# The skip term as a product with a diagonal on TensorE, the gate product on VectorE, the weighing of x on GpSimd, in a Mamba-2 block

## The chip, the cores and the metric

One core of one Trainium2 chip runs the whole program. The metric is device time in microseconds. The engines are PE (TensorE), DVE (VectorE), ACT (ScalarE), POOL (GpSimd) and SP (SyncE, which here only issues DMAs); each works off its own queue in order, and semaphores tie them together.

## The reference

The input is 8 sequences of 512 tokens with 128 channels. What matters here is the Mamba part:

```
x    = rmsnorm(layernorm(h));  proj = x @ in_proj_w          # z, xBC, dt
xBC  = silu(causal depthwise conv of width 4 over xBC)
xs   = x part, 32 heads of 64;  B, C: 8 groups of 64 states
dt   = softplus(dt_raw + dt_bias);  dA = exp(-exp(A_log) dt)
h_t  = dA_t h_(t-1) + (dt_t x_t) B_t ;   y_t = h_t . C_t
y    = y + D * xs                                            # the skip term
g    = y * silu(z);  g = g * rsqrt(mean(g^2) over groups of 256 + eps)
out  = residual + (g * gate_norm_w) @ out_proj_w
```

A feed-forward part with ternary weights, GELU and two layer norms follows. The change doesn't touch it.

## The kernel before, in words

A batch is one sequence. Its 2048 inner channels are 16 tiles of 128 channels (two heads of 64 each) by 512 tokens. The program works in slots, 16 to a batch and one for each such tile, four to a unit (r = 0 to 3). All the engines run the same slots with a function `slot(b, n)` each, and a tile passes through them with lags: projected and convolved, then four slots later transposed, scanned and its gate projected (`LAG_SSD`), after five its decays and matrices are made on POOL (`LAG_M`), after six its chunk states are built (`LAG_STATE`), after seven its y (`LAG_Y`), after eight the skip term, gate and square (`LAG_SUM`), then the norm, and after fifteen the out projection (`LAG_OUT`). Batches 1 to 6 run in a hardware loop (`Fori`); the first and the last ones are written out. Slots with r = 1 and 2 project two convolution tiles, those with r = 0 and 3 one (`PLAN`), and every slot projects one gate tile z. Each projection is three passes of 512 columns (`three_passes`, high and low parts).

In a slot PE does half of the transposes of x, the state products of the even blocks (`states(0)`, 64x64 tiles), the first projection, the other transposes, `states(1)`, then small transposes that differ by slot: C times B into `cbs` at r = 0, B into `bt` at r = 1, the norm factor into `rbs` at r = 2, the next batch's input in slot 7 and the result in slot 15 (`XN_SLOT`, `XO_SLOT`). Then, in an order that depends on the slot, a second projection if there is one, y within the blocks (`y_intra`, 32 records), the out projection, the variance at r = 0, the gate projection, and y from the states (`y_inter`, 28 records). The waits for y (`y_inputs`) are placed before the last pass of a two-tile slot's second projection, and before the out projection in the other slots.

DVE does the skip term (`skip`: D times x plus y, from PSUM, two instructions, one for the even and one for the odd blocks), the scan that makes the decay matrix `lm`, the weighing of x for the states (`weigh`: `xw`, out of PSUM), and then seven steps of the state recurrence (`state_step`) interleaved with the three convolution taps of each tile (`ORDER`). The state products of the next slot on PE wait for the last step. ACT starts each convolution (`start_tile`), ends it with SiLU (`finish_tile`), copies PSUM to SBUF, makes `xdt` (x times dt, eight pieces), the gate's SiLU and the square. POOL multiplies `lm` by `cbs`, y by the gate, makes `cdec`, applies the norm factor and sums squares. SP reloads `spread` (the decays, spread over partitions) when `cdec` has read it.

`y_bank[e]` are two PSUM banks; their left half holds y, their right half (`spare`) the small transposes. The ring of `lm` has eight places.

## Time and profile before

| | us |
|---|---|
| median of 3 runs | 1373.94 (1372.95 to 1377.06) |
| the profiled execution | 1385.78 |
| its span | 1384.0 |
| busy: PE / DVE / POOL / ACT | 1127.0 / 1080.2 / 897.2 / 789.1 |
| mean granted TensorE clock | 0.927 of full speed |

Busy time is the union of an engine's instructions in the profiled execution; it counts neither waits nor the issue of DMAs. Matmuls overlap one another in the records, so the time that PE needs for a group is read from the start of the group to the start of the next.

### The profile page before, as it was taken

To read this page: it belongs to the slowest core of one execution; us is meant where nothing else is said; L and a number is where in the kernel's file an instruction comes from. 1 tells how busy PE (TensorE), PEld (TensorE's weight loads), DVE (VectorE), ACT (ScalarE), POOL (GpSimd) and SP (SyncE) were. 2 spreads that over 40 slices of the span, in tenths; PEclk is the share of its full clock that TensorE was granted. 3 is DMA by queue.
4 is the path that set the end of the run, shared out by engine and by line. 5 is a ranking of instruction groups with operands and counts; after the bars stand their busy time and mean duration, and the time that the engine had idled before them with its cause. 6 is when DMAs were issued, how large, how long until landed. Compare 5 with 4: busy or idle time off the path is not lost. (4 is left out here: it accounts for less than half of the span.)

```text
span 1384.0 us, 43524 instructions
## 1 busy us (share of the span) xinstructions
PE 1127.0 (81%) x15222; PEld 772.6 (56%) x15222; DVE 1080.2 (78%) x2325; ACT 789.1 (57%) x2090; POOL 897.2 (65%) x848
## 2 busy tenths in 40 slices
PE   2447889888889879888989798979898999887687
PEld 1324666565556556555656566646565666553455
DVE  7737898887788868885888588868887888656895
ACT  2635666665566646663666466646665666542443
POOL 1632478786687758775878487857786788694231
PEclk9975899998999989997999799989999999896999
DMA  5432123222222222221322122222221321201211
GB/s 140 153 87 58 48 69 86 63 65 63 63 72 62 63 60 87 58 70 51 81 65 64 57 78 63 63 71 73 57 73 50 91 63 63 70 25 40 100 30 31
DMA packets 88881, 94.40 MB, mean 68 GB/s; under 512 B 22736, under 2 KB 66384, under 8 KB 88400
## 3 DMA queue, kind: packets, MB, share of 16 engines
q1 hardware_dynamic: 84432, 89.37, 22.9%
q8 instruction: 133, 2.18, 0.6%
q10 hardware_dynamic: 4224, 2.10, 0.5%
q14 instruction: 92, 0.75, 0.2%
HBM read 81.99 MB, written 9.44 MB: 66 GB/s over the span
## 5 line engine op out<-in xcount | busy, mean ns | idle before, releaser
L1067 DVE SCALAR_TENSOR_TENSOR conv<-bank,cw,conv 128x511 f32<-128x511 f32 (+2 forms) x576 | 426.8, 741 | 38.4 <-ACT conv L764 37.8
L764 ACT ACTIVATE conv<-bank,cb_bias,cw 128x512 f32<-128x512 f32 x192 | 149.1, 777 | 196.6 <-PE bank L1294 196.6
L619 POOL TENSOR_TENSOR gated<-gated,gate 128x512 f32<-128x512 f32 x128 | 163.8, 1280 | 100.6 <-DVE gated L1029 99.5
L864 ACT ACTIVATE xdt<-bank,dt_all 128x64 f32<-128x64 f32 x1024 | 222.4, 333 | 0.0
L1081 DVE SCALAR_TENSOR_TENSOR hpk<-hpk,pend,bank 128x64 f32<-128x64 f32 x768 | 210.4, 274 | 9.9
L1364 PE MATMUL bank<-gated,w_out 128*128 128x512 f32 x256 | 156.2, 695 | 63.8 <-ACT cbs L799 20.0
L612 POOL TENSOR_TENSOR lm<-lm,cbs 128x512 f32<-128x512 f32 x128 | 163.6, 1278 | 48.9 <-ACT cbs L799 37.0
L640 POOL TENSOR_TENSOR ssum<-ssum,sq 128x512 f32<-128x512 f32 x96 | 122.7, 1278 | 88.4 <-ACT sq L845 88.4
L1029 DVE SCALAR_TENSOR_TENSOR gated<-chan,dskip,bank 128x256 f32<-128x256 f32 x256 | 110.8, 474 | 88.1 <-PE bank L1484 80.1
L634 POOL TENSOR_TENSOR gated<-gated,rbs 128x512 f32<-128x512 f32 x128 | 163.7, 1280 | 13.2 <-ACT rbs L814 13.0
L1290 PE MATMUL bank<-xn_hi,w_hi 128*128 (+1 forms) x320 | 165.9, 518 | 7.3 <-PE bank L1473 3.3
L1342 PE MATMUL bank<-xw,bt 64*64 64x64 f32 x3584 | 167.7, 233 | 0.0
L629 POOL TENSOR_TENSOR cdec<-spread,chan 128x512 f32<-128x512 f32 x128 | 163.9, 1280 | 0.0
L1056 DVE TENSOR_TENSOR xw<-bank,wt_all 128x512 f32<-128x512 f32 x128 | 88.4, 690 | 91.5 <-PE bank L1375 88.8
L1342 PEld LDWEIGHTS bank<-xw,bt 64*64 64x64 f32 x3584 | 131.5, 141 | 46.8 <-issue 46.4
L1294 PE MATMUL bank<-xn_hi,w_lo 128*128 (+1 forms) x320 | 137.6, 430 | 22.3 <-DVE hpk L1081 13.4
L1043 DVE TENSOR_TENSOR_SCAN lm<-spread,bank 128x512 f32<-128x512 f32 x128 | 155.0, 1211 | 0.0
L1375 PE MATMUL bank<-ident_t,chan 128*128 128x128 f32 x512 | 108.7, 296 | 55.5 <-ACT xdt L864 22.1
L1484 PEld LDWEIGHTS bank<-cdec,hpk 64*64 64x64 f32 x3584 | 119.1, 139 | 59.4 <-issue 57.5
L1484 PE MATMUL bank<-cdec,hpk 64*64 64x64 f32 x3584 | 136.7, 226 | 0.5
L1291 PE MATMUL bank<-xn_lo,w_hi 128*128 (+1 forms) x320 | 133.0, 416 | 0.0
L784 ACT ACTIVATE chan<-conv 128x512 f32<-128x512 f32 x192 | 121.0, 630 | 19.3 <-issue 8.5
(175 smaller groups left out, 1613.7 us busy)
## 6 DMA issues: line engine op xcount, KB each, us to landing
spread<-decay_scratch SPq DMA_DIRECT2D x256, 128.0 KB, 3.3
spread<-product_scratch SPq DMA_DIRECT2D x256, 128.0 KB, 3.8
lm<-in_L_attn_in_proj_w SPq DMA_DIRECT2D x1, 2048.0 KB, 8.6
xn_scratch<-chan SPq DMA_DIRECT2D x4, 512.0 KB, 5.0
r_stage<-residual_scratch SPq DMA_DIRECT2D x8, 256.0 KB, 2.7
x_scratch<-r_stage SPq DMA_DIRECT2D x8, 256.0 KB, 3.6
cbs<-x_scratch SPq DMA_DIRECT2D x8, 256.0 KB, 3.0
gated<-x_scratch SPq DMA_DIRECT2D x1, 2048.0 KB, 8.9
```

The source lines that it names most:

```text
L612: gp.tensor_tensor(lm[:, at, :], lm[:, at, :], cbs[:, v % 2, :], ALU.mult).then_inc(m_done, 1)
L619: gp.tensor_tensor(gated[:, v % 2, mr, :], gated[:, v % 2, mr, :], gate[:, mr, :], ALU.mult).then_inc(gated_done, 1)
L629: gp.tensor_tensor(cdec[:, mr, :], spread[:, mr, 1, :], chan[:, chan_of(v, 1), :], ALU.mult).then_inc(cdec_done, 1)
L634: gp.tensor_tensor(gated[:, v % 2, m % R, :], gated[:, v % 2, m % R, :], rbs[:, :], ALU.mult).then_inc(normed, 1)
L864: act.activation(xdt[:, r, at:at + HP], xt_bank[:, at:at + HP], ACT.Copy, scale=dt_h).then_inc(xdt_done, 1)
L1043: V.tensor_tensor_scan(lm[:, m % (2 * R), :], spread[:, m % R, 0, :], seed_bank[:, :], 0.0, ALU.mult, ALU.add).then_inc(scanned, 1)
L1067: V.scalar_tensor_tensor(out=conv[:, ci % 4, shift:S], in0=tile_bank(b, n, t)[:, 0:S - shift], scalar=cw[:, q, t, KW - 1 - shift:KW - shif ...
L1081: V.scalar_tensor_tensor(out=hpk[:, m % 2, k, :], in0=hpk[:, m % 2, k - 1, :], scalar=pend[:, m % R, k:k + 1], in1=s_bank[:, NS * k:NS * k ...
L1290: MM(dst, wh, hi, start=True, stop=False)
L1342: last = MM(s_bank[half, NS * (2 * c + e):NS * (2 * c + e) + NS], bt[rows_e, c, half], xw[rows_e, m % R, P * c + HP * a:P * c + HP * a + H ...
L1364: MM(out_bank[:, :], w_out[:, m, :], gated[:, (m // R) % 2, m % R, :], start=(m == 0), stop=(m == SLOTS - 1)).then_inc(out_step, 1)
L1484: last = MM(y_bank[e][half, BLK * c:BLK * c + BLK], hpk[half, m % 2, k - 1, :], cdec[half, m % R, BLK * k:BLK * k + BLK], start=False, sto ...
```

## The change

The skip term becomes two fp32 matmuls on PE (`y_skip`, between `y_intra` and `y_inter`), with a diagonal matrix of D as the weights, one of 16, which ACT makes once in batch 0 and which lie in the upper half of `lm`; so the ring of `lm` has four places. DVE multiplies y in PSUM by the gate (`gate_y`) instead of adding the skip term, and POOL's gate product goes. POOL makes `xw` from `xdt` instead of DVE from PSUM, one slot later than before. The weight `wt_all` isn't multiplied by dt any more. PE's order becomes: out projection, all transposes of x, `states(0)`, first projection, `states(1)`, variance, small transposes, then the second projection or the gate projection with `y_inputs` before its last pass, `y_intra`, `y_skip`, `y_inter`, and the gate projection where it has not been done. ACT and POOL get new orders, SP waits for `pend`, and the scaling of the out weights moves from before the slots into batch 0.

```diff
-
-ORDER = {0: "0123456", 1: "0T12T34T56", 2: "0T1T2T3T4T56T"}
...
+        diag = lm[:, R:2 * R, :].rearrange("p a s -> p (a s)").rearrange("p (m d) -> p m d", d=P)
...
-                after(sp, cdec_done, SLOTS, b, m - R)
+                after(sp, pend_done, SLOTS, b, m - R)
...
-                    after(gp, scanned, SLOTS, bb, m)
-                    after(gp, cb_copied, 2 * UNITS, bb, 2 * v + 1)
-                    after(gp, spread_loaded[mr], 64 * UNITS, bb, 64 * v + 63)
-                    state_there(gp, bb, m - R)
-                    at = m % (2 * R)
-                    gp.tensor_tensor(lm[:, at, :], lm[:, at, :], cbs[:, v % 2, :], ALU.mult).then_inc(m_done, 1)
-                if yy is not None:
...
-                    after(gp, gate_done, SLOTS, bb, m)
-                    skip_there(gp, bb, m)
-                    gp.tensor_tensor(gated[:, v % 2, mr, :], gated[:, v % 2, mr, :], gate[:, mr, :], ALU.mult).then_inc(gated_done, 1)
...
-                    gp.tensor_copy(pend[:, mr, :].unsqueeze(2),
-                                   spread[:, mr, 1, :].rearrange("p (k i) -> p k i", i=BLK)[:, :, BLK - 1:BLK]).then_inc(pend_done, 1)
+                        gp.wait_ge(dtstep_a, 7)
+                    after(gp, scanned, SLOTS, bb, m)
+                    after(gp, spread_loaded[mr], 64 * UNITS, bb, 64 * v + 63)
                     after(gp, silu_done, NCONV, bb, CONV_ORDER.index((v, 1)))
                     after(gp, y_ready, SLOTS, bb, m - R)
                     gp.tensor_tensor(cdec[:, mr, :], spread[:, mr, 1, :], chan[:, chan_of(v, 1), :], ALU.mult).then_inc(cdec_done, 1)
+
+                    xdt_there(gp, bb, m)
+                    after(gp, s_ready, SLOTS, bb, m - R)
+                    wt_b = (wt_all[:, bass.ds(bb * CH, CH), 8 * v + mr:8 * v + mr + 5:4]
+                            .unsqueeze(3).broadcast_to([P, CH, 2, HP]))
+                    gp.tensor_tensor(xw[:, mr, :].rearrange("p (c a d) -> p c a d", c=CH, a=2),
+                                     xdt[:, mr, :].rearrange("p (c a d) -> p c a d", c=CH, a=2),
+                                     wt_b, ALU.mult).then_inc(xw_done, 1)
...
-                if yy is not None and yy[1] % R > 0:
-
-                    bb, m = yy
-                    after(gp, sq_done, SLOTS, bb, m)
-                    after(gp, ssum_step, 3 * UNITS, bb, 3 * (m // R) + m % R - 2)
-                    gp.tensor_tensor(ssum[:, m // R % 2, :], ssum[:, m // R % 2, :], sq[:, :], ALU.add).then_inc(ssum_step, 1)
...
+                if yy is not None and yy[1] % R > 0:
...
+                    after(gp, cb_copied, 2 * UNITS, bb, 2 * v + 1)
+                    state_there(gp, bb, m - R)
+                    gp.tensor_tensor(lm[:, mr, :], lm[:, mr, :], cbs[:, v % 2, :], ALU.mult).then_inc(m_done, 1)
+                    gp.tensor_copy(pend[:, mr, :].unsqueeze(2),
+                                   spread[:, mr, 1, :].rearrange("p (k i) -> p k i", i=BLK)[:, :, BLK - 1:BLK]).then_inc(pend_done, 1)
...
+            def scale_weights(n):
+
+                if n == 0:
+                    act.wait_ge(wo_loaded, 16 * 2 * UNITS)
+                    act.wait_ge(small_loaded, NSMALL * 16)
+                act.activation(w_out[:, n, :], w_out[:, n, :], ACT.Copy, scale=gnw[:, n:n + 1]).then_inc(wo_scaled, 1)
+                if n == 5:
+                    act.wait_ge(wlo, 4 * UNITS)
+                if 5 <= n < 13:
+                    for m in (2 * n - 10, 2 * n - 9):
+                        act.activation(diag[:, m, :], ident, ACT.Copy, scale=dskip[:, m:m + 1]).then_inc(diag_done, 1)
...
-                finish_tile(0)
-                if real:
-                    start_tile(PLAN[r][0])
-                finish_tile(1)
+                def square():
+
+                    if yy is not None:
+                        bb, m = yy
+                        skip_there(act, bb, m)
+                        v = m // R
...
+                if isinstance(b, int) and b == 0:
+                    scale_weights(n)
+                if not two:
+                    square()
+                if real:
+                    start_tile(PLAN[r][0])
+                if r == 0 and back(b, n, LAG_VAR) is not None:
...
-                if real and len(PLAN[r]) == 2:
-                    start_tile(PLAN[r][1])
...
+                if two:
+                    square()
+                if two and real:
+                    start_tile(PLAN[r][1])
                 if ssd is not None:
 
                     bb, m = ssd
-                    after(act, xw_done, SLOTS, bb, m)
+                    after(act, xt_ready, SLOTS, bb, m)
+                    after(act, xw_done, SLOTS, bb, m - 4)
...
+                    skip_there(act, bb, m - 4)
                     act.activation(gate[:, m % R, :], tile_bank(b, n, "z")[:, :], ACT.Silu).then_inc(gate_done, 1)
+                finish_tile(0)
+                finish_tile(1)
...
-                def skip():
+                def gate_y():
 
                     bb, m = yy
                     v, mr = divmod(m, R)
                     after(dve, y_ready, SLOTS, bb, m)
+                    after(dve, gate_done, SLOTS, bb, m)
                     for e in range(2):
-                        V.scalar_tensor_tensor(out=blocks(gated[:, v % 2, mr, :])[:, :, e, :],
-                                               in0=blocks(chan[:, chan_of(v, 2 + mr), :])[:, :, e, :],
-                                               scalar=dskip[:, m:m + 1],
-                                               in1=y_bank[e][:, 0:S // 2].rearrange("p (c s) -> p c s", s=BLK),
-                                               op0=ALU.mult, op1=ALU.add).then_inc(skipped, 1)
+                        V.tensor_tensor(blocks(gated[:, v % 2, mr, :])[:, :, e, :],
+                                        y_bank[e][:, 0:S // 2].rearrange("p (c s) -> p c s", s=BLK),
+                                        blocks(gate[:, mr, :])[:, :, e, :], ALU.mult).then_inc(skipped, 1)
...
-                    after(dve, y_ready, SLOTS, bb, m - 2 * R)
...
-                def weigh():
...
-                    after(dve, xt_ready, SLOTS, bb, m)
-                    after(dve, s_ready, SLOTS, bb, m - R)
-                    if isinstance(bb, int) and (bb, m) == (0, 0):
-                        dve.wait_ge(wt_ready, 1)
-                    wt_b = (wt_all[:, bass.ds(bb * CH, CH), 8 * mq + mr:8 * mq + mr + 5:4]
-                            .unsqueeze(3).broadcast_to([P, CH, 2, HP]))
-                    V.tensor_tensor(xw[:, mr, :].rearrange("p (c a d) -> p c a d", c=CH, a=2),
-                                    xt_bank[:, :].rearrange("p (c a d) -> p c a d", c=CH, a=2),
-                                    wt_b, ALU.mult).then_inc(xw_done, 1)
...
+                if not real:
+                    states(0, 2)
+                    batch_edges()
+                    states(3, 6)
+                elif len(PLAN[r]) == 1:
+                    t = PLAN[r][0]
+                    states(0, 2)
+                    batch_edges()
+                    one_tap(1, t)
+                    states(3, 4)
+                    one_tap(2, t)
+                    states(5, 6)
+                    one_tap(3, t)
+                else:
+                    t, u = PLAN[r]
+                    states(0, 1)
+                    one_tap(1, t)
+                    states(2, 2)
+                    one_tap(2, t)
+                    states(3, 3)
+                    one_tap(3, t)
+                    states(4, 4)
+                    one_tap(1, u)
+                    states(5, 5)
+                    one_tap(2, u)
+                    states(6, 6)
+                    one_tap(3, u)
...
-                def x_transposes(half):
+                def x_transposes():
 
                     bb, m = ssd
                     mq, mr = divmod(m, R)
-                    for c in range(2 * half, 2 * half + 2):
-                        if c == CH - 1:
-                            if st is not None:
-                                after(pe, s_low_done, SLOTS, *st)
-                            spare_free()
+                    after(pe, silu_done, NCONV, bb, CONV_ORDER.index((mq, 2 + mr)))
+                    xdt_there(pe, bb, m - 1)
+                    for c in range(CH):
                         last = TR(xt_bank[:, P * c:P * c + P], chan[:, chan_of(mq, 2 + mr), P * c:P * c + P], ident)
-                    if half == 1:
-                        last.then_inc(xt_ready, 1)
+                    last.then_inc(xt_ready, 1)
...
+                def y_skip():
+
+                    bb, m = yy
+                    after(pe, y_intra_done, SLOTS, bb, m)
+                    if isinstance(bb, int) and bb == 0:
+                        after(pe, diag_done, SLOTS, 0, m)
+                    for e in range(2):
+                        MM(y_bank[e][:, 0:S // 2], diag[:, m, :], blocks(chan[:, chan_of(m // R, 2 + m % R), :])[:, :, e, :],
+                           start=False, stop=False)
...
+                two = real and len(PLAN[r]) == 2
+                var = r == 0 and back(b, n, LAG_VAR) is not None
+                if st is not None:
+                    state_inputs()
+                out_projection()
+                if real and ssd is not None:
+                    x_transposes()
                 if st is not None:
                     states(0)
                 if real:
-                    project(b, n, PLAN[r][0])
-                if ssd is not None:
-                    x_transposes(1)
+                    project(b, n, PLAN[r][0], low_half_done)
                 else:
-                    if st is not None:
-                        after(pe, s_low_done, SLOTS, *st)
-                    spare_free()
-                    out_projection()
+                    low_half_done()
+                if not real and ssd is not None:
+                    x_transposes()
                 if st is not None:
                     states(1)
+                spare_free()
+                if var:
+                    variance()
                 small_transposes()
-                two = real and len(PLAN[r]) == 2
-                var = r == 0 and back(b, n, LAG_VAR) is not None
                 if two:
                     project(b, n, PLAN[r][1], y_inputs)
+                elif ssd is not None:
+                    gate_projection(y_inputs)
                 else:
                     y_inputs()
-                    if ssd is not None:
-                        out_projection()
                 if yy is not None:
                     y_intra()
-                    intra_finished()
+                    y_skip()
+                    y_inter()
                 if two and ssd is not None:
-                    out_projection()
-                if var:
-                    variance()
-                if ssd is not None and not two and not var:
-                    gate_projection()
-                if yy is not None:
-                    y_inter()
-                if ssd is not None and (two or var):
                     gate_projection()
```

## Rows read from the trace of the kernel before

**Rows 1.** The page's first part: busy us by engine (share of the span) xinstructions.

```profile
PE 1127.0 (81%) x15222; PEld 772.6 (56%) x15222; DVE 1080.2 (78%) x2325; ACT 789.1 (57%) x2090; POOL 897.2 (65%) x848
```

**Rows 2.** Stretches A:B: their length, busy us of each engine (xinstructions), clock, DMA share, GB/s.

```profile
384.40:528.10 143.70, 123.54 (x1828) 83.90 (x1829) 114.33 (x254) 87.44 (x243) 103.73 (x97) 0.95 0.23 66
...
961.70:1098.80 137.10, 122.13 (x1827) 82.80 (x1827) 114.19 (x253) 87.27 (x243) 103.50 (x97) 0.96 0.25 67
```

**Rows 3.** Timeline of PE over four slots: start, us, what, xcount [idle before <-releaser].

```profile
419.59 0.44 PE L1375 MATMUL bank<-ident_t,chan 128*128 128x128 f32 x2
...
423.50 1.13 PE L1364 MATMUL bank<-gated,w_out 128*128 128x512 f32 x2 [0.78 <-ACT cbs L799]
...
428.63 0.44 PE L1375 MATMUL bank<-ident_t,chan 128*128 128x128 f32 x2 [0.22 <-ACT xdt L864]
...
432.73 0.47 PE L1294 MATMUL bank<-xn_hi,w_lo 128*128 x1 [0.37 <-DVE hpk L1081]
433.13 0.69 PE L1473 MATMUL bank<-lm,xdt 64*64 64x64 f32 x32
433.92 1.12 PE L1364 MATMUL bank<-gated,w_out 128*128 128x512 f32 x2
434.97 1.03 PE L1484 MATMUL bank<-cdec,hpk 64*64 64x64 f32 x28
435.93 0.50 PE L1290 MATMUL bank<-xn_hi,w_hi 128*128 x1
...
436.75 0.44 PE L1375 MATMUL bank<-ident_t,chan 128*128 128x128 f32 x2
...
439.33 0.66 PE L1413 MATMUL bank<-ident_t,rexp 128*128 128x128 f32 x4
...
451.61 0.43 PE L1375 MATMUL bank<-ident_t,chan 128*128 128x128 f32 x2 [0.42 <-DVE hpk L1081]
```

**Rows 4.** Timeline of slot 7 in batch 2: ACT, DVE and PE.

```profile
412.69 0.66 ACT L819 ACTIVATE xn_hi<-bank 128x256 f32 x2 [0.16 <-PE bank L1418]
...
413.58 0.76 DVE L1095 TENSOR_TENSOR xn_lo<-bank,xn_hi 128x256 f32 x2 [1.32 <-ACT xn_hi L819]
...
414.46 1.12 PE L1364 MATMUL bank<-gated,w_out 128*128 128x512 f32 x2 [1.96 <-DVE xn_lo L1095]
...
416.39 0.79 PE L1290 MATMUL bank<-xn_hi,w_hi 128*128 x1
```

**Rows 5.** Around the back edge: timeline of DVE and PE, and a stretch of 2 us.

```profile
476.46 0.75 DVE L1067 SCALAR_TENSOR_TENSOR conv<-bank,cw,conv 128x511 f32<-128x511 f32 x1 [2.06 <-ACT conv L764]
...
491.44 0.68 PE L1375 MATMUL bank<-ident_t,chan 128*128 128x128 f32 x2 [4.74 <-ACT chan L784]
...
494.00:496.00 2.00, 2.00 (x30) 1.37 (x31) 0.65 (x1) 0.78 (x1) 0.96 (x1) 0.50 0.10 32
```

**Rows 6.** The chain of waits in the tail: start, us, what.

```profile
1271.36 0.86 PE bank L1364 x2
```

**Rows 7.** Groups by line and shape: xcount | busy us, mean ns of one | idle before.

```profile
L619 POOL TENSOR_TENSOR gated<-gated,gate 128x512 f32<-128x512 f32 x128 | 163.8, 1280 | 100.6 <-DVE gated L1029 99.5
...
L1029 DVE SCALAR_TENSOR_TENSOR gated<-chan,dskip,bank 128x256 f32<-128x256 f32 x256 | 110.8, 474 | 88.1 <-PE bank L1484 80.1 <-issue 7.9
...
L1056 DVE TENSOR_TENSOR xw<-bank,wt_all 128x512 f32<-128x512 f32 x128 | 88.4, 690 | 91.5 <-PE bank L1375 88.8 <-issue 0.8
...
L1364 PEld LDWEIGHTS bank<-gated,w_out 128*128 128x128 f32 x256 | 41.1, 201 | 85.8 <-issue 33.0 <-POOL gated L634 18.2 <-ACT cbs L799 11.0
```

**Rows 8.** Timeline of DVE in slot 14, the copy and the taps with a step between.

```profile
471.64 0.21 DVE L1078 COPY hpk<-bank 128x64 f32<-128x64 f32 x1
471.77 0.74 DVE L1067 SCALAR_TENSOR_TENSOR conv<-bank,cw,conv 128x511 f32<-128x511 f32 x1
...
472.62 0.74 DVE L1067 SCALAR_TENSOR_TENSOR conv<-bank,cw,conv 128x510 f32<-128x510 f32 x1
```

**Rows 9.** Timeline of ACT ahead of the slots, behind the scaling of w_out.

```profile
74.54 1.15 ACT L732 ACTIVATE cdec<-ssum,no_start 128x1024 f32<-128x1024 f32 x1 [7.67 <-DVE ssum L1013]
```

More of the change, by code:

```diff
@@ L285, in build @@
         skipped = sem("skipped")
-        gated_done = sem("gated_done")
+        diag_done = sem("diag_done")
         sq_done = sem("sq_done")
@@ L722, in _ @@
                     act.activation(src[1](w_hi), src[0], ACT.Copy).then_inc(whi, 1)
-            act.wait_ge(wo_loaded, 16 * 2 * UNITS)
-            act.wait_ge(small_loaded, NSMALL * 16)
-            for k in range(SLOTS):
-                act.activation(w_out[:, k, :], w_out[:, k, :], ACT.Copy, scale=gnw[:, k:k + 1]).then_inc(wo_scaled, 1)
             act.wait_ge(dtstep_v, DT_STEPS)
@@ L1083, in state_step, with batch_edges @@
                                                op0=ALU.mult, op1=ALU.add).then_inc(hstep, 1)
+                def batch_edges():
+                    if n == XN_SLOT and following(b) is not None:
+                        after(dve, hi_done, 2, b, 3)
+                        for e in range(2):
+                            half = slice(S // 2 * e, S // 2 * e + S // 2)
+                            V.tensor_tensor(xn_of(xn_lo, following(b))[:, half], spare(e), xn_of(xn_hi, following(b))[:, half].bitcast(F32),
+                                            ALU.subtract).then_inc(lo_done, 1)
+                    if n == XO_SLOT and back(b, n, SLOTS) is not None:
+                        bb, _ = back(b, n, SLOTS)
+                        after(dve, xo_ready, 1, bb, 0)
+                        dve.wait_ge(res_loaded, bb * 16 + 16)
+                        for e in range(2):
+                            xs = r_stage[:, 2 * e:2 * e + 2, :]
+                            V.tensor_tensor(xs, xo_half(b, e).rearrange("p (c d) -> p c d", d=DM), xs, ALU.add).then_inc(x1_done, 1)
@@ L1085, in slot, with states @@
+                def states(first, last):
+                    if state is not None:
+                        for k in range(first, last + 1):
+                            state_step(k)
                 if yy is not None:
-                    skip()
+                    gate_y()
                 if ssd is not None:
                     scan()
-                if ssd is not None:
-                    weigh()
-                if n == XN_SLOT and following(b) is not None:
-                    after(dve, hi_done, 2, b, 3)
-                    for e in range(2):
-                        half = slice(S // 2 * e, S // 2 * e + S // 2)
-                        V.tensor_tensor(xn_of(xn_lo, following(b))[:, half], spare(e), xn_of(xn_hi, following(b))[:, half].bitcast(F32),
-                                        ALU.subtract).then_inc(lo_done, 1)
@@ L1097, in slot @@
-                if n == XO_SLOT and back(b, n, SLOTS) is not None:
-                    bb, _ = back(b, n, SLOTS)
-                    after(dve, xo_ready, 1, bb, 0)
-                    dve.wait_ge(res_loaded, bb * 16 + 16)
-                    for e in range(2):
-                        xs = r_stage[:, 2 * e:2 * e + 2, :]
-                        V.tensor_tensor(xs, xo_half(b, e).rearrange("p (c d) -> p c d", d=DM), xs, ALU.add).then_inc(x1_done, 1)
-                taps = [(shift, t) for t in PLAN[r] for shift in range(1, KW)] if real else []
@@ L1105, in slot @@
[L1105 to L1109 removed]
+                if not real:
[11 more added lines that the diff above has]
+                    one_tap(3, t)
+                else:
+                    t, u = PLAN[r]
[11 more added lines that the diff above has]
+                    one_tap(3, u)
```

82 lines of the change are left out of this document (31 added, 51 removed).

## The prediction

> **What bounds the kernel now.** I read the busy shares first [rows 1]: PE 81%, DVE 78%, no engine full. Then the stretches of one batch each, from one scan of the first slot of a batch to the next [rows 2]: 143.7 us in the loop over batches, 137.1 us in the last batch but one, which has no back edge. So the loop decides, and the question is what ends last in a slot.
>
> PE in order of time over four slots of an undisturbed unit [rows 3] answers it. From the transposes at 419.59 us to those at 451.61 us is 32.0 us, so a batch of four such units would take 128.1 us and the remaining 15.6 us of the 143.7 are lost at two places. Inside the 32.0 us PE waits very little: 0.8 us for the cbs copy (423.50; from the end of the transposes for it), about 0.4 us for xdt at 428.63 (0.22 in the row, the rest is start-up), 0.5 us for the bt copy at 432.73 and the same for the rbs copy 8.1 us later, and 0.5 us before 451.61. That is 2.8 us, so PE has 29.2 us of work in 32.0 us. PE is the bound in all but name; DVE (114.3 busy of 143.7) and POOL (103.7) are looser [rows 2].
>
> The two places: in slot 7 the out projection waits 1.96 us for xn_lo, PE then runs at the lower clock (the first pass takes 0.79 us instead of 0.50) [rows 4], together about 3.5 us over a normal slot. And at the batch edge: DVE waits 2.06 us in slot 14 (its second accumulator comes behind the copy of the out bank), PE stands still 4.74 us at the back edge, and then runs at a granted clock of 0.50 (1.2 GHz) [rows 5]. That makes the other 12.1 us.
>
> **The change part by part.**
>
> *Skip term on PE.* Each slot gains two fp32 products, 256 columns wide, with 128x128 weights, in two records each: as many columns as one out projection, in four records instead of two. The trace has no such shape. From above: the out projection between small tiles costs 1.05 us from start to start (433.92 to 434.97) [rows 3]; if the four weight loads (0.20 us each by the mean of those of w_out [rows 7]) were not hidden at all, 1.6 us or somewhat more. From below: the out projection followed by another full-array product takes 0.86 us [rows 6]. I take 1.0 us, near the first row, since it stands between two groups of 64x64 products. The out projection itself moves ahead of the transposes, a full-array neighbour, and drops from 1.05 to about 0.9 us. Net 0.88 us a slot, 3.5 us a unit. PE waited for the end of y_intra before too (`intra_finished`), so that wait is not new.
>
> The Trainium skill ("TensorE: Matmul & The Clock Gate", Part 2) says that warm matmuls in a row start N/2.4 ns plus about 2.5 ns apart. By that rule four fp32 records of two streams each cost 0.87 us, and the sum below would be 17 us smaller, an estimate from that page of about 1396 us; the row for 512 columns (1.05 us for two records of two streams each, where the rule gives 0.86) [rows 3] speaks for the dearer value in this place.
>
> *Waits of PE.* The cbs wait was before the out projection; now two passes of the gate projection stand between, so of 0.8 us some 0.35 us is left. The xdt wait at 428.63 goes, because the out projection stands ahead of the transposes, and the one at 451.61 too. The waits for bt and rbs stay, 0.54 us each: the same two passes cover the same two copies. 2.8 us of waits become 1.4 us. Unit: 32.0 + 3.5 - 1.4 = 34.1 us.
>
> *Slot 7.* Now the four transposes of xn cost PE about 0.45 us, and its last pass waits for ACT's copy (0.66 us) and DVE's two subtractions (0.76 us) [rows 4], less the two passes: about 1.2 us. 1.65 us instead of 3.5 us, of which the lower clock was a part; I count none after so short a wait. *Edge.* The out projection at the head of the slot takes away the 2.06 us of slot 14; the transposes and wait of slot 15 leave about 1.1 us; the 4.74 us of the back edge stay, and the 10 us at half clock cost a PE without slack 5 us. 10.9 us instead of 12.1 us.
>
> *DVE.* Per slot it loses the weighing (0.69 us), and the two skip instructions (0.47 us each) [rows 7] become two products, for which the nearest row is xn_lo, also from PSUM and SBUF, two in 0.76 us [rows 4]: about 0.8 us a slot less. Worth nothing by itself, since PE is the bound; what matters is DVE's state chain. From the head of PE's slot to s_ready there were 2.6 us (436.75 to 439.33: transposes, both groups of states, three passes) [rows 3]; the out projection makes them 3.5 us. Then DVE does the copy (0.13 us to the next start), the first step and five pairs of tap and step at 0.85 us [rows 8]: 4.9 us in all with the semaphores. PE's next slot starts with the wait for that: 8.4 to 8.7 us from head to head in the slots with two tiles, where PE's own work with its wait is 8.1 us now (428.63 to 436.75) [rows 3] and 9.0 us then. Hidden, by little. Behind this wait on PE are the out projection and all the rest of the slot.
>
> *POOL.* One gate product less, one weighing more, at the 1.28 us of every two-input row of 512 columns there [rows 7]. It reads xdt of the slot before, which ACT ends about 0.4 us ahead of the slot's end, and PE wants the result at the head of the next slot: POOL does cdec and then the weighing, some 2.6 us into the slot. Hidden by over 4 us. If xdt were late, norm, ssum, the lm product and pend behind it would slip; y wants lm two slots later.
>
> *SP.* The reload of spread waits for pend, now POOL's last piece, instead of cdec: some 4 us later. The data is wanted by a scan about two slots on. Nothing. *lm ring of four:* the scan waits for y of the slot before, for which the gate product ahead of it waits anyway. Nothing. *Start:* the 16 scalings of w_out leave a place behind which ACT stood idle for 7.67 us [rows 9], so no gain; they and 16 diagonals go into batch 0 on ACT, which has the least to do of the three engines of the slots (87.4 busy of 143.7 in a later batch [rows 2]).
>
> **Sum.** 32 units at +2.1 us: +67. The first fifteen slots fill the pipeline and are bound by loads and latency: -6. Slot 7, seven times -1.85: -13. Five looped edges at -1.2 and two plain ones at -1.5: -9. Total +39 us. The profiled execution took 1385.8 us (span 1384.0), 12 us over the median of 1373.9; the difference is applied to the median: 1413 us, slower.
>
> **Rivals.**
> *A, faster side.* PE keeps its work in order and the waits left vanish: the copies of cbs, bt and rbs arrive behind the two passes in time, and the new products sit where PE would otherwise stand. For: the reordering aims the passes at each wait, and 26.8 us per batch of waits and slow clock (2.8 x 4 + 15.6) stand against 14 us of added work. Against: the same two passes left 0.54 us before. With no wait left the unit is 32.7 us, 32 x 0.7 - 28 = -6 us, and with the products at the row from below, 0.86 us [rows 6], another 18 us: 1374 - 24 = 1350 us. It decides below a remaining wait of 0.2 us a unit at my price of the products. Chance 0.18.
> *B, no difference.* Half of that: cheap products with waits, or dear ones without. 1374 us. Chance 0.1.
> *C, the state chain.* The second accumulator of a slot comes behind the square on ACT; if it reaches DVE 0.5 us late, the last steps slip, and PE's head wait with them: 64 slots at +0.5 us, +32 us on the forecast, 1445 us. For: the chain lies only some 0.3 us under PE's own work. Chance 0.12.
> *D, dear products.* Weight loads not hidden: 0.6 us x 128 = 77 us more, 1490 us. Against: loads of other groups run alongside PE. Chance 0.05.
> Forecast: 0.55, with its own range of 1395 to 1435 us.
>
> **How the numbers follow.** About 0.3% is what a measurement of this kernel can tell from no change. Slower: forecast, C and D, 0.72; within 0.3%: 0.1; faster: A, 0.18. The range reaches down into A and up to C: 1364 to 1444 us; outside are the lower half of A, the upper half of C, and D.
>
> **What would show it.** In the profile after: unit of 34 us from head to head of PE; the new products at 0.25 us a record; PE busy well over 85% of the span while DVE falls under 75%; in slot 7 a wait under 1.3 us and no fall of the clock; no DVE wait in slot 14; the back edge as before. Wrong if a unit takes under 33 us (A), if the wait at PE's head is for the last state step (C), or if the records take 0.4 us (D).

## The result and the profile after

The changed kernel takes 1426.04 us (median of 4, 1423.4 to 1430.8) against 1374.87 us for the kernel before: a ratio of 1.036, 95% interval 1.0308 to 1.0412. It is slower by 51 us. The forecast was 1413 us, slower, with 1395 to 1435 us as its own range.

The profiled execution of the kernel after took 1428.66 us (span 1426.9). The page's first part, as [rows 1]:

```profile
PE 1238.8 (87%) x15734; PEld 860.6 (60%) x15734; DVE 991.7 (69%) x2196; ACT 786.6 (55%) x2106; POOL 864.0 (61%) x848
```

PE gained 112 us of work, DVE lost 89. The stretches of one batch, from one y within the blocks to the next batch's (here the columns are as in [rows 2]): a looped batch, the last batch but one, the first batch, and 2 us behind the wait that stands below.

```profile
432.70:581.90 149.20, 138.14 (x1890) 95.77 (x1889) 103.52 (x237) 86.48 (x245) 99.48 (x97) 0.95 0.24 64
1033.50:1171.60 138.10, 132.45 (x1885) 91.98 (x1884) 102.03 (x234) 84.78 (x237) 97.37 (x94) 1.00 0.23 66
142.50:283.50 141.00, 132.19 (x1859) 92.41 (x1858) 102.45 (x234) 89.72 (x257) 89.81 (x89) 0.94 0.24 62
204.00:206.00 2.00, 2.00 (x21) 1.55 (x20) 0.00 (x0) 0.00 (x0) 2.00 (x2) 0.50 0.17 54
```

With both kernels cut at the same instruction, the whole difference of the traces (1426.9 - 1384.0 = 42.9 us) has these places: start +0.3, the first batch 129.3 to 141.0 (+11.7), five looped batches 721.2 to 750.0 (+28.7), the last but one 134.4 to 138.1 (+3.7), last batch and tail 256.8 to 255.3 (-1.5).

PE in order of time over a part of an undisturbed unit, which answers to [rows 3]:

```profile
441.94 0.69 PE L1497 MATMUL bank<-lm,xdt 64*64 64x64 f32 x32
442.73 1.13 PE L1519 MATMUL bank<-chan,lm 128*128 128x256 f32 x4
443.79 1.03 PE L1508 MATMUL bank<-cdec,hpk 64*64 64x64 f32 x28
444.75 1.12 PE L1391 MATMUL bank<-gated,w_out 128*128 128x512 f32 x2
445.71 0.60 PE L1400 MATMUL bank<-ident_t,chan 128*128 128x128 f32 x4
...
449.74 0.47 PE L1321 MATMUL bank<-xn_hi,w_lo 128*128 x1 [0.37 <-ACT bt L838]
...
453.76 1.02 PE L1391 MATMUL bank<-gated,w_out 128*128 128x512 f32 x2
454.62 0.60 PE L1400 MATMUL bank<-ident_t,chan 128*128 128x128 f32 x4
...
458.66 0.47 PE L1321 MATMUL bank<-xn_hi,w_lo 128*128 x1 [0.37 <-ACT rbs L846]
```

From start to start the new products (L1519, four records) take 442.73 to 443.79, 1.06 us. The out projection takes 0.96 us behind a group of 64x64 products (444.75 to 445.71) and 0.86 us behind a pass (453.76 to 454.62). The waits for xdt are gone, those for bt and rbs are where they were. From one y to the next the four slots take 9.19, 8.20, 8.92 and 7.88 us: 34.19 us a unit.

Three further places: PE in slot 15 of the first batch, PE in slot 7 (as in [rows 4]), and DVE between the scan and the first state step:

```profile
200.23 0.40 PE L1321 MATMUL bank<-xn_hi,w_lo 128*128 128x512 f32 x1
202.64 1.27 PE L1391 MATMUL bank<-gated,w_out 128*128 128x512 f32 x2 [2.01 <-ACT w_out L753]
203.70 1.06 PE L1400 MATMUL bank<-ident_t,chan 128*128 128x128 f32 x4
...
432.32 0.49 PE L1321 MATMUL bank<-xn_hi,w_lo 128*128 x1 [1.41 <-DVE xn_lo L1093]
...
448.41 0.22 DVE L1080 COPY hpk<-bank 128x64 f32<-128x64 f32 x1 [1.67 <-issue]
```

In the first batch the out projection waits 2.01 us for the last of the sixteen scalings of `w_out`; behind it the clock is at 0.50 (the stretch above), the transposes take 1.06 us instead of 0.60, and three slots take 12.87, 11.08 and 9.65 us, where the same three take 7.89, 9.27 and 8.27 us when nothing waits for the scaling (e4 below). DVE, which loses work by the change, stands still 1.67 us before the first state step, in the other slots much the same (226.9 us before 128 such copies).

### The profile page after: what moved, and what is told of

It is laid out like the page before. It is cut to its first block, busy times and chain, and to the rows that moved or that the text cites. A ratio compares the mean times of both kernels' runs of the same rounds, so it can differ in the third digit from the quotient of the medians.

```text
span 1426.9 us, 44626 instructions
## 1 busy us (share of the span) xinstructions
PE 1238.8 (87%) x15734; PEld 860.6 (60%) x15734; DVE 991.7 (69%) x2196; ACT 786.6 (55%) x2106; POOL 864.0 (61%) x848
## 4 chain that ended last, share of the span: by engine, by line
PE 72%; issue 9%; DVE 7%; ACT 5%; POOL 4%; SPq 1%; DMA 1%; ACTq 1%; POOLq 0%; DVEq 0%
PE bank L1519 10%; PE bank L1369 9%; PE bank L1391 8%; PE bank L1508 8%; PE bank L1321 7%; PE bank L1317 6%; PE bank L1497 6%; PE bank L1400 4%; PE bank L1318 3%; PE bank L1462 3%; PE bank L1423 2%; PE bank L1437 1%; POOL gated L625 1%; PE bank L1430 1%; ACT rbs L846 1%
## 5 line engine op out<-in xcount | busy, mean ns | idle before, releaser
L612 POOL TENSOR_TENSOR cdec<-spread,chan 128x512 f32<-128x512 f32 x128 | 163.9, 1280 | 37.7 <-DVE lm L1059 37.6
L1080 DVE COPY hpk<-bank 128x64 f32<-128x64 f32 x128 | 28.8, 225 | 226.9 <-issue 221.5
L1321 PE MATMUL bank<-xn_hi,w_lo 128*128 (+1 forms) x320 | 141.1, 441 | 40.4 <-ACT rbs L846 11.0
L1047 DVE TENSOR_TENSOR gated<-bank,gate 128x256 f32<-128x256 f32 x256 | 96.2, 419 | 109.9 <-PE bank L1508 92.1
L1391 PE MATMUL bank<-gated,w_out 128*128 128x512 f32 x256 | 145.2, 651 | 29.6 <-issue 20.1
L1519 PE MATMUL bank<-chan,lm 128*128 128x256 f32 x512 | 152.1, 421 | 11.3
L618 POOL TENSOR_TENSOR xw<-xdt,wt_all 128x512 f32<-128x512 f32 x128 | 136.0, 1063 | 21.1 <-ACT xdt L879 21.1
L632 POOL TENSOR_TENSOR rtok<-vtok,neghalf 128x8 f32<-128x8 f32 x32 | 52.7, 1648 | 143.4 <-ACT vtok L823 143.4
```

What stands on the lines that cost most here:

```text
L612: gp.tensor_tensor(cdec[:, mr, :], spread[:, mr, 1, :], chan[:, chan_of(v, 1), :], ALU.mult).then_inc(cdec_done, 1)
L1321: MM(dst, wl, hi, start=False, stop=True).then_inc(done, 1)
L1391: MM(out_bank[:, :], w_out[:, m, :], gated[:, (m // R) % 2, m % R, :], start=(m == 0), stop=(m == SLOTS - 1)).then_inc(out_step, 1)
L1519: MM(y_bank[e][:, 0:S // 2], diag[:, m, :], blocks(chan[:, chan_of(m // R, 2 + m % R), :])[:, :, e, :], start=False, stop=False)
```

## The experiments

Ratios are to the kernel before on the same chip; the changed kernel's is 1.036. A unit is four slots, from one y within the blocks to the next, away from slot 7 and the batch edge.

| kernel | median us | ratio, interval | unit us |
|---|---|---|---|
| e1 narrow product | 1357.78 | 0.9861, 0.9808 to 0.9914 | 32.4 |
| e10 the same, wait behind the out projection | 1344.12 | 0.9742, 0.971 to 0.9773 | 31.2 |
| e2 product twice | 1520.62 | 1.1017, 1.0987 to 1.1047 | 37.6 |
| e5 old order, with the product | 1473.85 | 1.0684, 1.0652 to 1.0716 | 34.7 |
| e7 wait behind the out projection | 1424.33 | 1.0315, 1.0278 to 1.0353 | 34.2 |
| e8 weighing on DVE | 1424.39 | 1.0323, 1.0261 to 1.0385 | 34.2 |
| e4 scaling early | 1414.61 | 1.0249, 1.022 to 1.0279 | 34.2 |
| e3 skip term on DVE | 1407.2 | 1.0211, 1.0163 to 1.0258 | 32.9 to 35.7 |
| e13 the same, PE waits for less | 1371.36 | 0.992, 0.9888 to 0.9953 | 31.9 to 33.6 |
| e9 the same, square later too | 1320.84 | 0.9564, 0.9528 to 0.9599 | 30.7 |
| e11 e9 with the gate product on POOL | 1322.59 | 0.9594, 0.956 to 0.9627 | 30.7 |
| e12 e9 with the scaling early | 1317.43 | 0.9558, 0.9529 to 0.9587 | 30.7 |

**What the product costs: less of it (e1), and twice (e2).** e1 leaves out the skip term for all but 8 columns, e2 adds it twice.

```
-                    for e in range(2):
-                        MM(y_bank[e][:, 0:S // 2], diag[:, m, :], blocks(chan...)[:, :, e, :], ...)
+                    MM(y_bank[0][:, 0:8], diag[:, m, :], chan[:, ..., 0:8], ...)     # e1
```

```
-                    for e in range(2):
+                    for e in (0, 1, 0, 1):                                           # e2
```

> The changed kernel with the two products of the skip term cut to one product of 8 columns (it leaves out the skip term for all but these columns). Theory (PE is the bound, its products cost 1.06 us a slot from start to start): the remaining product costs about 0.3 us, so PE saves some 0.75 us a slot; a unit of four slots goes from 34.2 to about 31.2 us, and the time from 1424 to about 1330 us. Rival C (the chain out projection, states, state steps holds the slots with two tiles at 8.4 to 8.7 us): these slots go from 8.9 to 8.6 us only, the unit to about 32.1 us, the time to about 1358 us, and PE's head waits for the last state step. Rival (PE isn't the bound): no change.

> The changed kernel with the two products issued twice (the skip term is then added twice). Theory (PE is the bound in every slot): every slot grows by another 1.0 us, the unit from 34.2 to 38.3 us, the time by 128 x 1.0 = 130 us to about 1555 us. Rival (part of the product's time lies in waits that PE has anyway): under 90 us more.

PE in e1, then in e2:

```profile
425.61 0.39 PE L1518 MATMUL bank<-chan,lm 128*128 128x8 f32 x2
425.92 1.03 PE L1508 MATMUL bank<-cdec,hpk 64*64 64x64 f32 x28
...
450.80 1.12 PE L1391 MATMUL bank<-gated,w_out 128*128 128x512 f32 x2 [0.39 <-DVE hpk L1083]
```

```profile
463.08 1.99 PE L1519 MATMUL bank<-chan,lm 128*128 128x256 f32 x8
465.01 1.03 PE L1508 MATMUL bank<-cdec,hpk 64*64 64x64 f32 x28
```

In e1 the product takes 0.32 us (425.61 to 425.92), 0.74 us less, and a unit should be 4 x 0.74 = 3.0 us shorter: 31.2. It is 32.4, since PE now waits for the last state step, the chain of rival C. In e2 the unit is 3.4 us longer: two pairs take 1.93 us, so the second one costs 0.87 us where the first costs 1.06. The Trainium skill ("TensorE: Matmul & The Clock Gate", Part 2) spaces warm matmuls by N/2.4 ns plus some 2.5 ns; a pair, counted as four records of two streams of 256 columns, comes to 0.87 us by that rule (an estimate from that page), and the second pair agrees with it. The first does not: the pair alone costs 0.19 us more between two groups of 64x64 products. That this is a fixed price of that place is argued and not shown; e1's 8 columns still take 0.32 us there. Units alone would make e2 32 x 3.43 = 110 us longer than the changed kernel, the spans differ by 88 (1515.3 and 1426.9): in four of the five looped batches the slot at the edge takes 15.0 to 15.3 us in place of 16.1 to 18.6, and the granted clock over the span is 0.964 against 0.942. The expectation (1555 us, a unit of 38.3) had neither that give-back nor the cheaper second pair.

**The state chain (e10, e7).** The same edit on e1 and on the changed kernel: PE's wait for the state's inputs stands behind the out projection.

```
+                out_projection()
                 state_inputs()
-                out_projection()
```

> The kernel with the narrow product (8 columns in place of 2 x 512; it leaves out the skip term but for these columns), with PE's wait for the state's inputs behind the out projection instead of ahead of it. Theory: with the product gone the state's chain holds PE's head (0.39 us before the out projection), so the later wait gives back 0.3 to 1 us a unit: 31.2 to 32.0, and 1320 to 1348 us against 1358 of e1. Rival: PE's own work was the bound and the wait moves to the state product: 1355 to 1361.

> The changed kernel with PE's wait for the state's inputs (the weighed x of the slot) behind the out projection instead of ahead of it, and nothing else. Theory: with the whole products PE's own work is the bound of a unit (34.19 us) and the wait had ended before PE came to it: the same unit and time, within 0.5% of the changed kernel (1420 to 1432 us). Rival (chain C): the state's chain holds PE there as it did in the kernel with the narrow product, which got 14 us from the same edit: 1408 to 1415 us.

On e1 it gives back 14 us and the unit is the 31.2 us that PE's own work makes. The unit alone is worth more, 32 x 1.13 = 36 us. Part of the difference goes to the clock: the slot behind slot 7 takes 10.05 us in e10 in all six batches that have the wait of 1.41 us there, and 8.45 us in e1 (granted clock in its first 4 us: 0.66 to 0.70 against 1.00). On the changed kernel it gives nothing that can be told (the intervals overlap, slots of 9.19, 8.20, 8.89 and 7.88 us). So the chain is real: it holds three of the four slots of e1 (8.90, 8.51 and 7.49 us, where e10 has 8.45, 8.17 and 7.16; the fourth is 7.46 in both). In the changed kernel these three take 9.19, 8.92 and 7.88 us, so the chain lies 0.3 to 0.4 us a slot beneath PE's work, and rival C does not decide there.

**What the new order is worth (e5), and the weighing's place (e8).** e5 is the kernel before, in its order of PE's work and with its weighing on DVE, with the products on PE and the gate product on DVE. e8 is the changed kernel with `weigh` on DVE again.

```
+        for e in range(2): MM(y_bank[e]..., diag[:, m, :], chan...)   # e5: behind y_intra, else as before
+        V.tensor_tensor(gated..., y_bank[e]..., gate..., ALU.mult)    # e5: for skip; POOL's gate product gone
```

```
-        gp.tensor_tensor(xw..., xdt..., wt_b, ALU.mult)               # e8
+        V.tensor_tensor(xw..., xt_bank..., wt_b, ALU.mult)
```

> The kernel before in its own order with one part of the change alone: the skip term as products on PE behind y_intra, the gate product on DVE (POOL's goes), ring of four for lm. Weighing stays on DVE, the orders of PE, ACT and POOL stay. Theory (the products cost their full 1.06 us a slot, the reordering takes back about 1.4 us of waits a unit and 3 us a batch): the unit goes from 32.0 to about 36 us, the time to about 1500 us, some 75 us above the changed kernel. Rival (DVE and POOL, relieved, give back part of it in the old order too): 1420 to 1450 us, that is, the reordering is worth little.

> The changed kernel with the weighing of x back on VectorE, which reads it from PSUM where the transposes put it (as in the kernel before), in the new order; POOL then does 1.06 us a slot less and VectorE about 0.65 us a slot more. Theory: neither engine is the bound of a unit, so it stays at 34.19 us and the time within 0.5% (1420 to 1432 us). Rival: POOL's work beside VectorE's products slows them, or POOL ends last before PE in slot 7: the time falls to 1400 to 1415 us; or VectorE's scans come late: it rises above 1435 us.

PE's waits in e5, and its place behind the product (compare 451.61 in [rows 3]), then e8's page:

```profile
447.90 0.44 PE L1372 MATMUL bank<-ident_t,chan 128*128 128x128 f32 x2 [0.23 <-ACT xdt L862]
...
470.12 1.13 PE L1493 MATMUL bank<-chan,lm 128*128 128x256 f32 x4
...
472.84 0.44 PE L1372 MATMUL bank<-ident_t,chan 128*128 128x128 f32 x2
...
476.74 1.12 PE L1361 MATMUL bank<-gated,w_out 128*128 128x512 f32 x2 [0.78 <-ACT cbs L797]
```

```profile
PE 1231.5 (87%) x15734; PEld 856.4 (60%) x15734; DVE 1067.1 (75%) x2325; ACT 787.8 (55%) x2106; POOL 735.3 (52%) x720
```

e5 is 94 us over the kernel before (0.0684 x 1374.87), the changed kernel 49.5: the new orders, the weighing and the later scaling together earn 44.5 us. e5 misses its expectation (about 1500 us, a unit of 36) by 26 us: its unit is only 2.7 us above the 32.0 of the kernel before and not 4. The waits for cbs and xdt are still there, but the one of 0.42 us for the last state step ahead of the transposes (472.84) is gone, and the product with a full-array group beside it makes the stretch from y within the blocks to y from the states only 0.7 to 0.9 us longer a slot. e8 shows that in the new order the weighing's place earns none of it: DVE is 75 us busier (1067.1), and the slots are the same to 0.03 us. The product's 94 us are lessened, not hidden, by the reordering. Per unit the order is worth 0.5 us; most of the rest lies between units: from y to y across slots 14 and 15 a looped batch of e5 takes 13.0 to 13.9 us and the changed kernel 9.17, across slots 6 and 7 it is 11.3 to 11.6 and 9.95.

**The first batch (e4).**

```
-        act.activation(w_out[:, n, :], w_out[:, n, :], ACT.Copy, scale=gnw[:, n:n + 1])
+        for k in (2 * n, 2 * n + 1) if n < 8 else ():
+            act.activation(w_out[:, k, :], w_out[:, k, :], ACT.Copy, scale=gnw[:, k:k + 1])
```

> The changed kernel with ScalarE's sixteen scalings of w_out done two a slot in slots 0 to 7 of the first batch instead of one a slot. Theory: the first batch grew by 11.7 us since the out projection of its slot 15 waits 2.01 us for the last scaling and PE's clock is at 0.50 for some 13 us after it; with the wait gone the stretch there runs at full clock and the kernel takes 5 to 9 us less: 1424 us or so goes to 1415 to 1419. Rival: the clock falls there for the edge's other waits anyway, and only the 2 us go, or nothing (within 0.2%).

PE at the same place, and the first batch's stretch:

```profile
201.69 0.39 PE L1322 MATMUL bank<-xn_hi,w_lo 128*128 128x512 f32 x1
201.92 1.02 PE L1392 MATMUL bank<-gated,w_out 128*128 128x512 f32 x2
202.78 0.60 PE L1401 MATMUL bank<-ident_t,chan 128*128 128x128 f32 x4
```

```profile
144.00:276.90 132.90, 126.09 (x1860) 88.71 (x1860) 102.47 (x234) 87.44 (x248) 89.94 (x89) 0.99 0.26 65
```

The wait is gone, the clock stays up (0.99 over the batch, 0.94 in the changed kernel), and the batch takes 132.9 us instead of 141.0. The kernel's ratio falls to 1.0249, with intervals apart. A wait of 2.01 us cost 8.1, of which the lower clock behind it is the larger part.

**The skip term back on DVE, in the new order (e3), and what held it (e13, e9).** e3 takes the products off PE again: DVE does D times x plus y from PSUM as before, and behind the scan the product with the gate, both inputs in SBUF; the weighing stays on POOL, the out projection stands between y within the blocks and y from the states in every slot, and ACT copies the out bank at the head of slot 15. e13 lets PE write into `y_bank` as soon as DVE has read it; e9 moves the square of one-tile slots on ACT behind the tile's start too.

```
 def spare_free():                                                    # e13 and e9
-    skip_there(pe, *(back(b, n, LAG_Y + 1) or ...))                   # waits for the product with the gate
+    after(pe, diag_done, 2 * SLOTS, sb_, 2 * sm_ + 1)                 # waits for the skip instructions alone
-                if not two: square()                                  # e9
                 if real: start_tile(PLAN[r][0])
+                if not two: square()
```

> The changed kernel's order, weighing on POOL and ring of four, but the skip term back on DVE (two scalar_tensor_tensor as before, then the scan, then one product of 512 columns with the gate), no product with the diagonal on PE, the out projection back between the two parts of y, and the copy of the out bank at the head of slot 15. Theory (PE's own work decides, the gain of the reordering is real and was buried under the products): PE loses 1.06 us a slot and the state chain 0.9 us, the unit is 30 to 31 us, the time 1300 to 1330 us, under both kernels. Rival (DVE becomes the bound: 0.8 + 1.2 + 0.65 + 5.4 = 8.0 us in slots with two tiles, 6.1 in the others, with start-up waits 8.5 and 6.8): unit of 31 to 32 us, about 1345 us. Rival (the reordering gives nothing): about 1374 us.

> The kernel with the skip term on VectorE and the gate product on VectorE behind the scan (e3), but PE's variance product and next y wait only until VectorE has read both halves of y, not for the gate product behind, and ScalarE's square stands behind the first tile's start. Theory: in e3 the wait of 1.35 us for the gate product and the clock fall that followed it cost about 1.6 us a unit; the unit goes from 33.3 to 31.7 us and the kernel from 1407 to 1340 to 1355 us, faster than the kernel before. Rival: VectorE is the bound (two-tile slots of 8.1 us, the gate product of 1.42 us beside POOL): unit 32.8 or more, 1385 to 1405 us.

> The kernel with the skip term on VectorE (e3, 1407 us) with one edit alone: PE's variance product and next y wait only until VectorE has read both halves of y. ScalarE's square stays ahead of the tile's start. Theory: that wait of 1.35 us and the fall of the clock behind it make all of the difference between 1407 us and the 1321 us of the kernel with both edits: 1315 to 1330 us. Rival: half of it came from the square's place, which delays the convolution that VectorE waits for (0.5 to 0.7 us a slot): 1345 to 1385 us.

e3 misses its expectation by 60 us and more. Its PE, DVE and POOL at r = 0, and the stretch behind:

```profile
463.36 1.26 POOL L625 TENSOR_TENSOR gated<-gated,rbs 128x512 f32<-128x512 f32 x1
...
463.75 1.42 DVE L1053 TENSOR_TENSOR gated<-gated,gate 128x512 f32<-128x512 f32 x1
...
465.49 1.05 PE L1468 MATMUL bank<-blockones,ssum 128*128 128x2 f32 x8 [1.35 <-DVE gated L1053]
...
469.58 2.08 PE L1397 MATMUL bank<-gated,w_out 128*128 128x512 f32 x2
```

```profile
468.00:471.00 3.00, 2.91 (x35) 1.57 (x35) 1.65 (x4) 2.53 (x10) 3.00 (x4) 0.56 0.00 0
```

The product with the gate starts 0.39 us after POOL's norm product and lasts 1.42 us; PE's variance waits 1.35 us for it though its bank was read long before; then the clock falls to its lower level and the out projection takes 2.08 us instead of 1.13. The slot at r = 0 takes 9.9 to 11.4 us in most units. e13 takes that wait away and gets 40 us (0.0291 of 1374.87), not all of the difference to e9: the rival of e13's expectation holds. What is left in e13, on ACT and PE:

```profile
451.54 0.63 ACT L800 ACTIVATE ssum<-gated 128x512 f32<-128x512 f32 x1 [3.33 <-DVE gated L1053]
...
452.74 0.26 ACT L823 ACTIVATE vtok<-bank,eps_c 128x8 f32<-128x8 f32 x1
...
453.05 0.50 PE L1323 MATMUL bank<-xn_hi,w_hi 128*128 x1 [1.05 <-ACT vtok L823]
```

ACT's square waits 3.33 us for DVE, the reading of the variance stands behind it, and PE behind that: 1.05 us, and again the lower clock. e9 moves the square and gets the other 49 us (the square was moved only together with the shorter wait, never alone); it is better than its own expectation (1340 to 1355), which allowed for a slower unit. In e9, the same place on DVE and POOL, then the page's first part:

```profile
439.94 0.78 DVE L1053 TENSOR_TENSOR gated<-gated,gate 128x512 f32<-128x512 f32 x1
...
440.13 1.72 POOL L625 TENSOR_TENSOR gated<-gated,rbs 128x512 f32<-128x512 f32 x1
```

```profile
PE 1113.4 (85%) x15222; PEld 757.9 (58%) x15222; DVE 1081.8 (82%) x2324; ACT 780.3 (59%) x2090; POOL 885.2 (67%) x848
```

The unit is 30.7 us against 32.0 of the kernel before, and the kernel is 4.4% faster than it.

**Which engine bounds it now (e11), and both edits (e12).** e11 gives the product with the gate back to POOL; e12 is e9 with the early scaling of e4.

```
-                    V.tensor_tensor(gated..., gated..., gate..., ALU.mult)            # e11
+                    gp.tensor_tensor(gated..., gated..., gate..., ALU.mult)
```

> As the kernel with the banks free early, but the gate product back on POOL (behind the passes' work, in place), so that the skip term is the only thing that moved back. Theory that VectorE is the bound of the two-tile slots there: 1 us a slot leaves VectorE, unit 31 to 31.7, 1320 to 1345 us. Rival: POOL with both the gate product (1.2 us or more) and the weighing (1.06 us) is full in two-tile slots (above 7.9 us) and the unit is 32.5 or more, 1375 us or above.

> The kernel with the skip term on VectorE and the banks free early (1320.84 us), with ScalarE's scalings of w_out two a slot in slots 0 to 7 of the first batch. Theory: the first batch there takes 123.7 us from its first y to the second batch's and its edge still waits 2.0 us for the last scaling, with slots of 9.70 and 8.36 us behind it; 2 to 8 us go: 1312 to 1319 us. Rival: nothing, since only one slot (9.70 us in place of 8.3) is long there: 1319 to 1322 us.

```profile
PE 1123.2 (85%) x15222; PEld 764.9 (58%) x15222; DVE 1007.3 (76%) x2196; ACT 778.7 (59%) x2090; POOL 1025.2 (78%) x976
```

This is e11's page: 74 us less on DVE and 140 more on POOL, and every undisturbed slot as in e9 (8.28, 7.29, 8.04 and 7.04 us). So neither engine bounds e9, and PE is what is left. No run changes PE's work in e9, but its rows speak for it: in an undisturbed unit PE waits only for bt and rbs, 0.37 us each by the rows, and the unit is 3.5 us shorter than the changed kernel's, which is what the products were priced at, net. The time is in my theory's range, but its reason, and the rival's, named the wrong engine. e12 can't be told from e9: its first batch takes 121.8 us against 123.7, the intervals overlap. The two are the best versions found.

## Why the prediction was right

*PE is the bound in all but name.* Right, and shown by e2, e10, e7 and e8: from the changed kernel on, a unit follows PE's work one for one (3.4 us for the second pair, 3.0 for the narrow one), and moving 75 us of work between DVE and POOL changes nothing.

*The product, 1.0 us; net 0.88 us a slot.* 1.06 us, and the out projection 0.96 and 0.86 us instead of 1.05. Rival D (dear products) is out: a record takes 0.26 us. That the row for 512 columns speaks for more than 0.87 us in this place was right: in e2 the excess comes with the first pair and not with the second.

*Waits 2.8 to 1.4 us; unit 34.1 us.* 34.19 us. Rival A is out: the copies for bt and rbs still come 0.37 us late by the rows, with the gap around them 0.54, as before. The credit for the waits was in part misplaced: the 0.5 us ahead of 451.61 go in e5 too, without the new order.

*Slot 7: +1.65 us without a fall of the clock.* 9.95 us instead of 7.88, +2.07: the wait is 1.41 us by its row and was to be under 1.3. In five of the six batches with this wait the clock stays up; in one it falls (a slot of 10.74 us behind instead of 9.2). *Edge.* DVE's wait in slot 14 is gone; slot 7 and edge together cost the looped batch shown 149.2 - 4 x 34.19 = 12.4 us and the mean of the five 13.2 us, where 1.65 + 10.9 = 12.55 was forecast.

*The state chain, hidden by little.* Right: it is hidden by 0.3 to 0.4 us a slot, and it becomes the bound as soon as PE loses the product.

*POOL, the lm ring, SP: nothing.* Nothing in the slots of a looped batch points to them, and e8 shows it for the weighing, which takes POOL 1.06 us and not the 1.28 I took.

**Two terms were mis-sized, and they cancel.** Spread over the places of the section on the result, my sum reads (us):

| place | my sum | measured |
|---|---|---|
| start | -1.0 | +0.3 |
| first batch | +1.9 | +11.7 |
| five looped batches | +26.8 | +28.7 |
| last batch but one | +6.9 | +3.7 |
| last batch and tail | +4.7 | -1.5 |
| all | 39 | 42.9 |

The first is the start. "They and 16 diagonals go into batch 0 on ACT, which has the least to do" was costed at nothing, because I looked at ACT's load and not at who waits: the last scaling is due in slot 15, just when the first out projection wants it. The first batch grew by 9.8 us more than my share for it; e4 shows 8.1 of them. The second is the edge without a loop, -1.5 us each: in the last two batches the slot with DVE's wait in slot 14 took 12.77 and 13.16 us and takes 9.18 and 9.23 now, so these two places came out 9.4 us below my sum. That the total of 39 lies so near 42.9 is therefore luck; what the sum got right by its reasons is the looped batches, which are two thirds of it.

**And the step from trace to median.** I applied the sum to the median as if the 12 us of the profiled execution above it were in both kernels. The profiled execution of the kernel after is only 2.6 us above its median, that of before 10.9, so the medians differ by 51 us. Where those 8 us lie is not settled. The kernel before took 1376.2 to 1390.1 us in fifteen later executions, the shorter ones mostly at a granted clock of 0.93 to 0.94 and the longest at 0.927, as in the profiled one; so it may have stood longer at the lower clock than the typical execution.

## What to carry to other kernels

When an engine is the bound, a cheap instruction put on it costs nearly its full length; idle time on another engine, even 30% of the span, pays for nothing. Before you move work to relieve an engine, ask which one sets the slot. With the skip term left on DVE, much the same reordering was 2.1% slower than the kernel before (e3) and, with one wait and one place in ACT's order mended, 4.4% faster (e9); with it on PE, whose rows show neither of these two waits, it is 3.6% slower. And when a variant disappoints, look at what its first waits are *for*: one wait that asked for more than it needed, and one instruction that stood ahead of work it had nothing to do with, made 89 us of difference between e3 and e9.

## What the hardware showed

- **Products of DVE and POOL exclude one another.** DVE's product with both inputs in SBUF takes 0.67 us alone, 1.42 us when POOL's norm product has started 0.39 us before it, and when DVE is first, POOL's takes 1.72 us instead of 1.28 (e9, POOL 0.19 us behind). In the changed kernel the product with the gate reads y from PSUM and POOL's norm products take 1.28 us. The Trainium skill ("SBUF — State Buffer", Who interferes with whom) states it as a lock: a VectorE instruction with two SBUF inputs and a GpSimd one that reads SBUF exclude each other, and the one that starts second waits. The rows agree in the main; a full wait would make the two longer ones about 0.1 us longer still.
- **The clock can fall after a wait of about one microsecond.** It did in e13 after 1.05 us and in e3 after 1.35 us, in most units.
- **The same wait is followed by either level.** In slot 7 of batches 1 to 6 PE waits 1.41 us for xn_lo in five kernels alike. In the 4 us from y of that slot on the granted clock stays at 1.00 in all six batches of e1; it falls in one of six in the changed kernel, in three in e4, which does the same work there, in four in e2 and in all six in e10. It costs 1.3 to 1.6 us each time. What else it takes is open.
- **With the product doubled the clock is higher at the edge, not in slot 7.** The granted clock over the span is 0.964, the slot at the batch edge is over 1 us shorter in four of five looped batches, and 22 of 110 us of added work do not show in the span; but behind slot 7 the clock falls more often than in the changed kernel.
